# Eigenvector setup of a graph layer on one core: recurrence steps reordered, ScalarE's loop unrolled, three transposed buffers, a later count and basis, reciprocal deviations in four parts

## The reference, cut to what matters

```python
h = relu(layernorm(x))                       # x (128, 120, 1024)
degv = A.sum(0) + A.sum(1) - diag(A); Ln = D^-1/2 (diag(degv) - A) D^-1/2   # 120 x 120
_, U = eigh(Ln)                              # 120 eigenvectors
agg = einsum('vn,bvd->bnd', U, h)
out = relu(agg @ W1 + b1) @ W2 + b2          # then a non-local block on out:
g, phi = maxpool2(conv(out)); theta = conv(out)
z = bn(wo @ (softmax(theta phi) g)) + out
result = x + einsum('nv,bvd->bnd', U, z) + z
```

## Time and profile before

| | |
|---|---|
| median of 3 runs | 3327.8 us |
| the profiled execution | 3326.99 us, span 3325.2 us |
| busy, share of the span: PE, DVE, ACT, POOL | 95%, 70%, 73%, 57% |
| first product of the main stage (PE L818) starts | 638.86 us |
| the chain that ended last, by engine | PE 80%, DVE 16%, issue 3% |

### The profile page before, as it was taken

How to read it: one execution, slowest core, us unless ns; L and a number is a source line. 1 busy time by engine, 2 the same in 40 slices (tenths; PEclk the granted TensorE clock), 3 DMA queues, 4 the chain that set the end, 5 groups by cost and what they waited for, 6 DMA issues and landing times.

```text
span 3325.2 us, 65809 instructions
## 1 busy us (share of the span) xinstructions
PE 3168.9 (95%) x16040; PEld 2546.6 (77%) x16040; DVE 2322.8 (70%) x6363; ACT 2411.2 (73%) x4380; POOL 1890.5 (57%) x1718
## 2 busy tenths in 40 slices
PE   6888987799999999999999999999999999999997
PEld 4677776577777777777777777777777777777775
DVE  7998888766666666666666666666666666666664
ACT  6889999666666666666666666666666666666665
POOL 3222211166666666666666666666666666666665
PEclk9999999899999999999999999999999999999998
DMA  3334443212222222222222222222222222222222
GB/s 100 93 100 108 111 114 104 66 50 72 73 73 73 73 73 73 74 72 72 72 72 72 72 72 72 72 72 72 72 72 72 72 72 73 74 72 72 73 72 66
DMA packets 111574, 256.21 MB, mean 77 GB/s; under 512 B 47500, under 2 KB 49797, under 8 KB 111493
## 3 DMA queue, kind: packets, MB, share of 16 engines
q1 hardware_dynamic: 111493, 255.25, 28.2%
HBM read 190.69 MB, written 63.44 MB: 76 GB/s over the span
## 4 chain that ended last, share of the span: by engine, by line
PE 80%; DVE 16%; issue 3%; POOL 1%; DMA 0%; ACT 0%; DVEq 0%; POOLq 0%; ACTq 0%
PE ps_M L802 8%; PE ps_M L803 8%; PE ps_M L804 8%; PE ps_S L879 7%; PE ps_E L802 7%; PE ps_O L802 7%; PE ps_E L803 7%; PE ps_O L804 7%; PE ps_E L804 7%; PE ps_O L803 7%; PE ps_M L863 3%; DVE ST L1133 1%; DVE row L1019 1%; DVE rown L1033 1%; DVE zt L1023 1%
## 5 line engine op out<-in xcount | busy, mean ns | idle before, releaser
L505 POOL TENSOR_TENSOR p_lo<-p,p_hi 128x512 fp32r<-128x512 f32 x1024 | 1383.5, 1351 | 929.4 <-ACT p_hi L656 928.3
L651 ACT ACTIVATE p<-ps_E 128x512 f32<-128x512 f32 x1024 | 613.6, 599 | 332.4 <-PE ps_E L804 307.4
L1410 DVE TENSOR_REDUCE nmx<-ps_S 128x1 f32<-128x512 f32 x1024 | 658.6, 685 | 125.2 <-PE ps_S L879 123.9
L656 ACT ACTIVATE p_hi<-p 128x512 fp32r<-128x512 f32 x1024 | 647.2, 632 | 32.6
L802 PE MATMUL ps_E<-o_hi,Q_hi 123*128 123x512 f32 x1024 | 426.9, 417 | 0.0
L802 PE MATMUL ps_O<-p_hi,v_hi 128*121 128x512 f32 x1024 | 407.3, 398 | 4.2 <-POOL p_lo L505 4.2
L804 PE MATMUL ps_O<-p_lo,v_hi 128*121 128x512 f32 x1024 | 406.7, 397 | 0.0
L804 PE MATMUL ps_E<-o_lo,Q_hi 123*128 123x512 f32 x1024 | 404.2, 395 | 0.0
L803 PE MATMUL ps_E<-o_hi,Q_lo 123*128 123x512 f32 x1024 | 404.2, 395 | 0.0
L803 PE MATMUL ps_O<-p_hi,v_lo 128*121 128x512 f32 x1024 | 404.1, 395 | 0.0
L1390 DVE TENSOR_REDUCE gf<-ps_M 128x256 f32<-128x512 f32 x256 | 177.1, 692 | 262.6 <-PE ps_M L804 262.6
(11 more groups left out here) (364 smaller groups left out, 5947.3 us busy)
## 6 DMA issues: line engine op xcount, KB each, us to landing
rbc<-r_dram SPq DMA_DIRECT2D x128, 484.0 KB
xin<-in_x_dram SPq DMA_DIRECT2D x128, 480.0 KB, 4.2
xt<-in_x_dram SPq DMA_DIRECT2D x128, 480.0 KB, 5.0
out_dram<-y SPq DMA_DIRECT2D x128, 480.0 KB, 3.7
o_hi<-mrow SPq DMA_DIRECT2D x256, 2.0 KB
dcol<-y SPq DMA_DIRECT2D x128, 4.0 KB, 2.0
r_dram<-rcol SPq DMA_DIRECT2D x128, 4.0 KB, 1.4
W1s<-in_L_gnn_W_dram SPq DMA_DIRECT2D x1, 512.0 KB, 4.3
```

Of the source, the lines that this page charges most:

```text
L505: pool.tensor_tensor(p_lo[:, c % 4, :], p[:, c % 4, :], p_hi[:, c % 4, :].bitcast(F32), ALU.subtract).then_inc(plo_sb, 1)
L651: act.activation(p[:, c % 4, :], ps_E[c % 2][:, :], ACT.Exp).then_inc(p_sb, 1)
L656: act.activation(p_hi[:, c % 4, :], p[:, c % 4, :], ACT.Copy).then_inc(phi_sb, 1)
L1410: dve.tensor_reduce(nmx[:, c:c + 1], ps_S[SBANK[c]][:, :], AX.X, ALU.max, negate=True).then_inc(max_sb, 1)
```

## The change

In `minors` the difference `SP` of a step is issued before the shifted diagonals and the rescaling of that step; the scale reaches the rows one step later than before. `fT` has three buffers, and the scratch `junkx` lies in the last four parts of `P1`. ScalarE's 132 slots are all written out; in slot 127 the sum of squares stands behind the copy of slot 125. The copy of `EB` and `DE` and the sum over `wn` change places. The count is added up at the start of slot 102, and all three `basis` products stand behind the last product with W1. `W2hi` is made before the wait for `basis(1)`. GpSimd makes the deviations in parts of 64, 32, 16 and 16 columns, and does its first two `fetch` before it waits for `setup_done`.

```diff
-            junkx = eb("junkx", [N, D], BF16)
-            fT = eb("fT", [128, 2, KC * N])
+            junkx = P1[0:N, (B - 4) * H:B * H].bitcast(BF16)
+            fT = eb("fT", [128, 3, KC * N])
...
             rstds(0, B // 2)
+            rstds(B // 2, B * 3 // 4)
+            rstds(B * 3 // 4, B * 7 // 8)
+            pool.wait_ge(wy_ps, WY_P(7) + 1)
+            pool.memset(xt[0:1, :, :], 0.0).then_inc(xt_free, 1)
             pool.wait_ge(dve_out, 5)
...
-            pool.wait_ge(wy_ps, WY_P(7) + 1)
-            pool.memset(xt[0:1, :, :], 0.0).then_inc(xt_free, 1)
-            rstds(B // 2, B)
-            pool.wait_ge(rstd_done, 2)
-            pool.wait_ge(setup_done, 1)
+            rstds(B * 7 // 8, B)
+            pool.wait_ge(rstd_done, 4)
+            pool.wait_ge(p1_done, B)
+            pool.wait_ge(b1_in, 16)
...
             def turn(b, par):
+                if isinstance(b, int) and b == 0:
+                    pool.wait_ge(setup_done, 1)
...
             def b_ft(s, par):
                 act.wait_ge(tr_done, s + 1)
-                late(act, w1_done, s - 1)
+                late(act, w1_done, s - 2)
...
             def b_p1(s, par):
                 act.wait_ge(w1_done, s + 1)
+                if s == B - 4:
+                    act.wait_ge(sq_done, B)
...
-            for k in range(4):
-                slot(k, k % 2)
-            rounds(act, 4, WY_SLOT, slot)
-            for k in range(WY_SLOT, B + 4):
-                slot(k, k % 2)
-                if k < WY_SLOT + WY_STEPS:
+            for k in range(B + 4):
+                slot(k)
+                if WY_SLOT <= k < WY_SLOT + WY_STEPS:
                     factor(k - WY_SLOT)
...
-                if (i + 1) % UNITS == 0 and (i + 1) // UNITS - TAIL_AT in range(3):
-                    basis((i + 1) // UNITS - TAIL_AT)
+                if i == TAIL_AT * UNITS - 1:
+                    basis(0)
+            basis(1)
+            basis(2)
...
+                    need(turned)
+                    made = did(T(SP[:, s + 1, :, :], ST[:, :, :], SM[:, s % 2, :, :], ALU.subtract))
+
+                    if s % 2 == 0:
+                        need(rows)
+                    elif s + 2 < HALF:
+                        rows = shifted(s + 2)
                     phase = (s - 8) % 8 if 8 <= s < 54 else 8
-                    if s % 2 and s + 2 < HALF:
-                        rows = shifted(s + 2)
...
-                        rows = did(T(SA[:, s + 1, :, :], SA[:, s + 1, :, :], size.unsqueeze(2).to_broadcast([N, 2, K]), ALU.mult))
-                    need(turned)
-                    made = did(T(SP[:, s + 1, :, :], ST[:, :, :], SM[:, s % 2, :, :], ALU.subtract))
-                    if s % 2 == 0:
-                        need(rows)
+                        scaled = did(T(SA[:, s + 2, :, :], SA[:, s + 2, :, :], size.unsqueeze(2).to_broadcast([N, 2, K]), ALU.mult))
+                    elif phase == 5 and s > 8:
+                        need(scaled)
...
+            i_hi = did(dve.tensor_copy(W2hi[:, :], W2f[:, :]))
+            dve.wait_ge(pe_out, 6)
+            mark(dve.tensor_copy(Uaug[0:N, :], ps_up[0:N, 0:N]))
...
-TAIL_AT = B
+TAIL_AT = B + 2
-GRID_AT = 99
+GRID_AT = 102
```

More of the change, by code:

```diff
@@ L550, in b_p1, with slot @@
                 act.wait_ge(w1_done, s + 1)
-                act.activation(P1[0:N, bass.ds(s * H, H)], ps_m[par][0:N, 0:H], ACT.Copy).then_inc(p1_done, 1)
-            def slot(k, par):
-                fixed = isinstance(k, int)
-                if not fixed or k < B:
+                if s == B - 4:
+                    act.wait_ge(sq_done, B)
+                act.activation(P1[0:N, s * H:(s + 1) * H], ps_m[par][0:N, 0:H], ACT.Copy).then_inc(p1_done, 1)
+            def slot(k):
+                par = k % 2
+                if k < B:
                     b_relu(k, par)
+                if k < B - 1:
                     b_sq(k, par)
-                if not fixed or 0 <= k - 2 < B:
+                if 0 <= k - 2 < B:
                     b_ft(k - 2, par)
-                if not fixed or k + 1 < B:
+                if k == B - 1:
+                    b_sq(k, par)
+                if k + 1 < B:
                     act.wait_ge(sq_done, k + 1)
                     b_sum(k + 1, 1 - par)
-                if not fixed or 0 <= k - 4 < B:
+                if 0 <= k - 4 < B:
                     b_p1(k - 4, par)
@@ L695, in product @@
                     late(pe, p1_done, s - 1)
-                last = mm(ps_m[par][0:N, 0:H], fT[:, par, c * N:(c + 1) * N], W1s[:, c, :],
+                last = mm(ps_m[par][0:N, 0:H], fT[:, s % 3, c * N:(c + 1) * N], W1s[:, c, :],
                           start=(c == 0), stop=(c == KC - 1))
@@ L788, in _ @@
                 if i == GRID_AT * UNITS:
-                    pe.wait_ge(wn_ready, 1)
+                    pe.wait_ge(wn_ready, 3)
                     for j in range(1, 3):
@@ L1067, in _ @@
             dve.wait_ge(params, 16 * PARAMS)
+            dve.tensor_reduce(wn[:, :, N:NO], wn[:, :, 0:N], AX.X, ALU.add).then_inc(wn_ready, 1)
             dve.wait_ge(pe_out, 4)
-            mark(dve.tensor_copy(EB[:, 1:N + 1], ps_up[0:N, N:2 * N]))
-            step(dve.tensor_copy(DE[:, 0:N], ps_up[0:N, 0:N]))
-            dve.tensor_reduce(wn[:, :, N:NO], wn[:, :, 0:N], AX.X, ALU.add).then_inc(wn_ready, 1)
+            dve.tensor_copy(EB[:, 1:N + 1], ps_up[0:N, N:2 * N]).then_inc(wn_ready, 1)
+            dve.tensor_copy(DE[:, 0:N], ps_up[0:N, 0:N]).then_inc(wn_ready, 1)
+            dve.wait_ge(wn_ready, 3)
             d_ = DE[:, 0:N]
@@ L1115, in weighed @@
                 def weighed(s):
-                    q = s - 13
+                    q = s - 14
                     if q >= 0 and q % 8 < 2 and q < 48:
@@ L1150, in minors @@
                         need(sized)
-                        sized = did(T(SW[:, :, :], E2P[:, s + 2:s + 4, :], size.unsqueeze(1).to_broadcast([N, 2, 2]), ALU.mult))
+                        sized = did(T(SW[:, :, :], E2P[:, s + 3:s + 5, :], size.unsqueeze(1).to_broadcast([N, 2, 2]), ALU.mult))
                     elif phase == 4:
-                        need(rows)
                         need(sized)
-                        rows = did(T(SA[:, s + 1, :, :], SA[:, s + 1, :, :], size.unsqueeze(2).to_broadcast([N, 2, K]), ALU.mult))
-                    need(turned)
-                    made = did(T(SP[:, s + 1, :, :], ST[:, :, :], SM[:, s % 2, :, :], ALU.subtract))
-                    if s % 2 == 0:
-                        need(rows)
+                        scaled = did(T(SA[:, s + 2, :, :], SA[:, s + 2, :, :], size.unsqueeze(2).to_broadcast([N, 2, K]), ALU.mult))
+                    elif phase == 5 and s > 8:
+                        need(scaled)
                 need(made)
@@ L1341, in _ @@
             dve.tensor_copy(VT[:, :], ps_up[0:N, 0:N]).then_inc(dve_out, 1)
-            dve.wait_ge(pe_out, 6)
-            step(dve.tensor_copy(Uaug[0:N, :], ps_up[0:N, 0:N]))
-            T(Cop[0:N, 2 * H + 1:OPS], ps_up[0:N, N:2 * N], ident[0:N, 0:N], ALU.add).then_inc(dve_out, 1)
             def split(hi, lo, full):
@@ L1348, in split @@
                 mark(T(lo, full, hi.bitcast(F32), ALU.subtract))
-            split(W2hi[:, :], W2lo[:, :], W2f[:, :])
+            i_hi = did(dve.tensor_copy(W2hi[:, :], W2f[:, :]))
+            dve.wait_ge(pe_out, 6)
+            mark(dve.tensor_copy(Uaug[0:N, :], ps_up[0:N, 0:N]))
+            T(Cop[0:N, 2 * H + 1:OPS], ps_up[0:N, N:2 * N], ident[0:N, 0:N], ALU.add).then_inc(dve_out, 1)
+            need(i_hi)
+            mark(T(W2lo[:, :], W2f[:, :], W2hi[:, :].bitcast(F32), ALU.subtract))
             split(Qwhi[:, :], Qwlo[:, :], wn[:, 0, :])
```

10 lines of the change are left out of this document (5 added, 5 removed).

## The result

The changed kernel takes 3320.1 us (median of 12 runs, 3318.67 to 3321.68), the kernel before 3328.47 in 12 runs beside it: a ratio of 0.9976, 95% interval 0.9969 to 0.9983, that is 5.7 to 10.3 us less and by the medians 8.4. (0.2% of this kernel is 6.7 us, so the interval reaches to both sides of that border.) The profiled execution took 3320.95 (before 3326.99), its span 3319.2 (3325.2), 6.0 less. The first product of the main stage starts at 632.19, 6.67 earlier than the 638.86 of the earlier trace rows; from there to the end of the span it is 2687.0 us, before 2686.4. So the profile's whole gain lies in setup, where the prediction put it.

What follows compares the result with a forecast made beforehand. The prediction took setup as the bound, with VectorE's recurrence chain narrowly last: 12.0 us (two passes) + 2.25 (the end) - 7.8 (the later count) gives 6.5 less, 3321.3 us from 3327.8, range 3318.5 to 3325.5.

Steps and rivals of the forecast that it cites:

- list of signs: What the later profile would show if the forecast were right or wrong, such as step lengths, idle times and start instants.
- A pass saves 6.0 us: VectorE's recurrence: issuing SP earlier shortens odd and rescaling steps, saving 5.5 to 6.6 us per pass, taken as 6.0.
- S = 0: First rival's extreme: the reorder saves nothing per pass, time 3333.3 us; chance 0.06 for a saving S under 2.8.
- VectorE resumes 7.8 later: VectorE's wait before Cop for the count's product, now in slot 102: resumes at 510.3 to 510.4 against 502.57.
- The 0.9 us that ScalarE should have gained before slot 94: ScalarE's slots: gain from written-out slots and third fT buffer together, 0.9 us, with 0.6 and 2 as ends.
- The 0.3 for the third buffer: ScalarE's slots: the third fT buffer removes b_ft's wait for the product before it, worth 0.3 us.
- The 0.6 to 0.9 for the written-out loop: ScalarE's slots: without the loop's branch, 0.06 to 0.10 us less per pair of slots, 0.6 to 0.9 in all.
- Z at 626.4: End of VectorE's setup chain: Z moves from 630.64 to 626.4, by 7.8 us later count less 12.0 for two passes.
- Products with W1 done at 625.8: End of ScalarE's and TensorE's setup chain: through about 625.8, 0.9 us ahead of basis(0) at 626.7.
- third rival: ScalarE becomes the bound at the end of setup: 3322.2 us without its 0.9 gain, 3324 with late code; chance 0.2.
- From Z to the main stage 5.95: End of setup: Z to the main stage's first product takes 5.95 us instead of 8.22, 2.25 less.
- First product at 632.3: Start of the main stage: its first product comes at 632.3 against 638.86, 6.5 us less.

Runs made afterwards that it cites:

- old-order run: The changed kernel with the old instruction order in the recurrence steps, everything else kept: 3331.16 us, ratio 1.0012 to the kernel before.
- basis apart: The changed kernel with the three basis products behind each of the last three products with W1, as before: 3320.68 us, ratio 0.9983.
- two halves: The changed kernel with GpSimd's deviations in two halves, the last of 64 columns, as before: 3322.35 us, ratio 0.9983.
- order only: The kernel before with only the new order within the recurrence steps, rescaling included: 3320.66 us, ratio 0.9977.
- square first: The changed kernel with slot 127's sum of squares ahead of the copy of slot 125, as before: 3319.44 us, ratio 0.9979.
- two buffers: The changed kernel with two fT buffers again instead of three: 3321.04 us, ratio 0.9977.
- all three: The changed kernel with the count at slot 99, unread products around the main stage's start and unread transposes in the first six reflections: 3314.84 us, ratio 0.9961.

## Why the prediction was right, and where its steps were off

The prediction said 3321.3, range 3318.5 to 3325.5; measured 3320.1. The border of 0.2% runs between the two, and it fell on the faster side, to which 0.45 had been given. The path was not the one it had named: it said that VectorE's chain would stay the last, and ScalarE's was, which the list of signs had as one of being wrong (TensorE coming from a product straight to `basis(0)`). That the number came out all the same is in part luck, because the two chains end 0.4 us apart.

- **A pass saves 6.0 us.** 6.21, 6.48 and 6.31 were measured; steps of 0.53 and 0.55 as worked out. The scaled row and the reciprocal hide too: their steps take 0.48 and 0.47 us, before 0.71 and 0.61.
- **The skill's rule on draining** ("VectorE: DVE Perf Modes", section "The DRAIN you can't avoid") would have made S = 0 as the prediction read it. Small independent operations start 0.12 us after one of 0.20, in the new order as in the earlier trace rows, and the old-order run shows what S = 0 costs. The same section also says that a next operation which isn't held starts earlier; these rows agree with that sentence, and the prediction had left it out.
- **VectorE resumes 7.8 later.** 8.49. The 0.9 us that ScalarE should have gained before slot 94 were 0.45 at slot 82 and were used up by a late load of x. The 0.3 for the third buffer were about right (0.3 to 0.5 in its run). The 0.6 to 0.9 for the written-out loop were too much: the 12 slots from 82 to 94 take 51.43 to 51.47 us with it (but for the late load) and 51.68 to 51.71 in the three kernels with the loop, 0.04 for each pair of slots.
- **Z at 626.4.** 626.18: 0.7 more of delay, 0.8 more of saving in the two passes, and 0.2 in between.
- **Products with W1 done at 625.8.** This is the step that failed: they ended at 627.1 (621.61 + 5.47), and `basis(0)` started at 626.9, in the overlap of TensorE's products. ScalarE's last slot came 5.26 earlier and not 6.1 (no lead), and the order in slot 127 gave 0.63 and not 1.1, because the copy to P holds these products back anyway. So the third rival came true in its mildest form: ScalarE became the bound by 0.4 us, which costs 0.2 against the forecast's 626.7 for `basis(0)`.
- **From Z to the main stage 5.95.** 6.01, of which 0.4 is the wait for TensorE. From `Z` that is 2.21 less, where the sum had 2.25; from `basis(0)` on it is 5.27, before 7.88, 2.61 less. The two parts that I tried singly give 0.94 (basis apart) and 0.67 (two halves).
- **First product at 632.3.** 632.19. The rest of the span grew by 0.6, within the 1.5 put on the clock.

The number is right to 0.1 us in the profile, but it was summed along one chain: 12.0 + 2.25 - 7.8, VectorE's. The runs show that with the faster passes ScalarE and TensorE set the end by themselves, wherever the count stands: undone, the late count gives 15.5 us of VectorE's chain back and none of the time. Along ScalarE the gain reads: 5.26 at slot 127 (the stall of the earlier trace rows and what was left of the lead), 0.63 in the order of that slot, and 0.75 behind its products (638.86 - 633.0 of the prediction, against 632.19 - 627.08), 6.6 together. The stall goes as soon as either the first pass is shorter ("order only") or the count is later ("old order", 146.59 us from slot 94 to 127); but with the later count and the old order TensorE waits 12 us for VectorE. So the order in the steps carries nearly the whole gain; the other parts add at most 0.5 us to it and, without it, don't make the kernel faster.

The median fell by 8.4 where the profiled execution fell by 6.0. Of that, 0.5 may be the late load; the rest is within what executions vary by and was not taken apart.

## What to carry to other kernels

Before pricing a change along the chain that ends last, price the second chain with the same care: here both meet within 1 us, and a term of 7.8 us in the sum had no effect, because it moved an instant that the other chain covered. In a step of small dependent operations on VectorE, put the independent ones between the result and the one that waits for it. Where TensorE stands idle before a new stage, look at the granted clock behind it: here, filling the gaps with products that nobody reads gave 6 to 8 us, nearly as much as the whole change.

## What the runs showed of the hardware that was not expected

- **The low clock outlasts the idle stretch by far.** Behind 2.6 us of idleness the level was 0.5 for 13.7 us, although TensorE was busy for 10.33 of 13.66 us in it, then full for a moment and low for 6.8 us more. It cost 6 to 7 us in the pair of the change and in that of the kernel before. I had put 5 us on it and had not thought of it as something to be had.
- **A slow start, and a record of the clock that begins at its end.** The row product of a reflection takes 0.74 to 0.76 us for the first six to eight reflections and 0.46 after. The view gives PEclk as 1.00 throughout, but the trace's list of clock levels has no entry before 41.55 us in the change, 40.23 with "square first", 46.3 with "two buffers", "two halves" and "all three", and 52.53 with "order only". Its first entry is full speed, and the view counts time without an entry as full. In all 14 profiles the row product is slow before that instant and fast behind it (in the kernel before one lies across it, at 41.52 with the first entry at 42.02, and takes 0.69); in "order only":

```profile
47.33 0.74 PE L722 MATMUL ps_up<-zs,cs 1*120 1x114 f32 x2
52.93 0.46 PE L722 MATMUL ps_up<-zs,cs 1*120 1x113 f32 x2
```

  So the slow start is in all likelihood the low level, and its end the rise. It moves everything behind it by up to 3.5 us: the `zs` of the eleventh reflection starts at 56.96 to 60.48. This may be a good part of the 3 to 5 us by which runs of one kernel differ, but only one execution of each kernel is profiled. What decides when the rise comes stays open: filler work of two kinds did not bring it forward, and in "order only" TensorE was busy without a break from 36 to 52 us before it came. The Trainium skill ("TensorE: Matmul & The Clock Gate", section "Seeing it yourself") warns that the recorded events of the clock have been seen to be unreliable; here the entries that there are agree with the durations, and only the time before the first is missing.
- **A load of x can be late beside an instruction fetch.** The load for slot 83 took 5.5 us where others take about 4.2, with a fetch of instructions in the same microseconds; ScalarE lost 0.57. It was seen once, and that the fetch was the cause is argued, not shown.
